# Late output pieces and probability transposes brought together behind the third chunk of a turn

## The reference

```
a = einsum('bqd,bkd->bqk', layernorm(x), ctx)    # ctx: 1 x 25088 x 2048
e = softmax(a, axis=-1)
x = x + einsum('bqk,bkd->bqd', e, ctx)
```

## Time and profile before

| what | value |
|---|---|
| time, median of 3 runs | 2503.16 us (2502.03 to 2505.08) |
| the profiled execution: its time | 2499.3 us |
| the profiled execution: span, first to last instruction | 2497.7 us |
| mean granted clock of TensorE | 0.996 |
| TensorE busy | 2447.4 us, 98% of the span |
| TensorE weight loads | 2008.0 us, 80% |
| VectorE busy | 1944.8 us, 78% |
| GpSimd busy | 1418.9 us, 57% |
| ScalarE busy | 1093.8 us, 44% |
| chain that ended last | 93% TensorE |

### The profile page before, as it was taken

How to read it: one execution, slowest core, us unless ns; L and a number is a source line. 1 busy time by engine, 2 the same in 40 slices (tenths; PEclk the granted TensorE clock), 3 DMA queues, 4 the chain that set the end, 5 groups by cost and what they waited for, 6 DMA issues and landing times.

```text
span 2497.7 us, 36098 instructions
## 1 busy us (share of the span) xinstructions
PE 2447.4 (98%) x11446; PEld 2008.0 (80%) x11446; DVE 1944.8 (78%) x2702; ACT 1093.8 (44%) x1577; POOL 1418.9 (57%) x1056
## 2 busy tenths in 40 slices
PE   6999999999999999999999999999999999999799
PEld 5888888888888888888888888888888888877577
DVE  8788788787888878878788787888888878774356
ACT  4444444444444444444444444444444444333443
POOL 2766666666665665655556556466555655652341
PEclk9999999999999999999999999999999999999899
DMA  9988878888788888888988888888888889779633
GB/s 231 250 222 208 229 204 229 218 207 229 205 230 226 212 212 215 218 220 213 219 213 206 220 218 214 211 217 218 218 214 214 205 218 226 199 165 169 136 121 100
DMA packets 421112, 518.22 MB, mean 207 GB/s; under 512 B 54407, under 2 KB 296071, under 8 KB 418441
## 3 DMA queue, kind: packets, MB, share of 16 engines
q1 hardware_dynamic: 411080, 475.66, 78.1%
q0 software_dynamic: 9984, 41.95, 5.0%
HBM read 488.71 MB, written 28.84 MB: 207 GB/s over the span
## 4 chain that ended last, share of the span: by engine, by line
PE 93%; DMA 2%; DVE 2%; POOL 1%; issue 1%; ACT 1%; SPq 0%; POOLq 0%; ACTq 0%
PE ps L1451 30%; PE ps L1453 30%; PE ps L1452 30%; PE ps L1460 2%; DMA tr<-wt_dram 1%; POOL nat_lo L613 1%; DMA raw<-in_ctx_dram 1%; DMA x_in<-in_x_dram 0%; PE ps L1678 0%; PE ps L1751 0%; PE ps L1624 0%; PE ps L1479 0%; DVE tr L1072 0%; DVE acc L1197 0%; PE ps L1573 0%
## 5 line engine op out<-in xcount | busy, mean ns | idle before, releaser
L613 POOL TENSOR_TENSOR nat_lo<-raw,nat_hi 128x512 fp32r<-128x512 f32 x784 | 1169.7, 1521 | 867.8 <-ACT nat_hi L773 833.8
L1076 DVE TENSOR_TENSOR ch_lo<-tr,ch_hi 128x512 fp32r<-128x512 f32 x784 | 842.3, 1074 | 364.9 <-ACT ch_hi L762 364.8
L762 ACT CAST ch_hi<-tr 128x512 fp32r<-128x512 f32 x784 | 477.5, 621 | 810.3 <-PE ps L1453 804.0
L1451 PE MATMUL ps<-ch_hi,xt_hi 128*128 128x512 f32 x1696 | 678.3, 400 | 11.7 <-DVE ch_lo L1242 5.0
L1453 PE MATMUL ps<-ch_hi,xt_lo 128*128 128x512 f32 x1696 | 664.3, 392 | 0.0
L1452 PE MATMUL ps<-ch_lo,xt_hi 128*128 128x512 f32 x1696 | 663.3, 391 | 0.0
L1451 PE MATMUL ps<-nat_hi,pt_hi 128*128 128x512 f32 x1568 | 611.6, 390 | 4.6 <-DVE pt_lo L1017 4.6
L1453 PE MATMUL ps<-nat_hi,pt_lo 128*128 128x512 f32 x1568 | 610.2, 389 | 0.0
L1452 PE MATMUL ps<-nat_lo,pt_hi 128*128 128x512 f32 x1568 | 610.1, 389 | 0.0
L1072 DVE STREAM_TRANSPOSE tr<-quart 128x512 f32<-128x512 f32 x784 | 547.2, 698 | 1.0 <-DMA quart<-in_ctx_dram 1.0
L773 ACT CAST nat_hi<-raw 128x2048 fp32r<-128x2048 f32 x196 | 374.6, 1911 | 200.8 <-PE ps L1453 189.2
(11 more groups left out here) (200 smaller groups left out, 1312.1 us busy)
## 6 DMA issues: line engine op xcount, KB each, us to landing
quart<-in_ctx_dram SPq DMA_DIRECT2D x392, 512.0 KB, 8.4
raw<-in_ctx_dram SPq DMA_DIRECT2D x196, 1024.0 KB, 8.1
wq_in<-in_L_attn_Wq_dram POOLq DMA_DIRECT2D x16, 1024.0 KB, 6.4
win<-in_L_ffn_W_base_dram SPq DMA_DIRECT2D x64, 256.0 KB, 6.7
tr<-wt_dram POOLq DMA_DIRECT2D x64, 256.0 KB, 3.2
wt_dram<-stage SPq DMA_DIRECT2D x32, 256.0 KB, 5.5
wt_dram<-stage_b SPq DMA_DIRECT2D x32, 256.0 KB, 10.3
wq_dram<-wq_out POOLq DMA_DIRECT2D x16, 256.0 KB, 2.3
```

What stands on the lines that cost most here:

```text
L613: last = pool.tensor_tensor(nat_lo[:, j, t], raw[:, j % 2, t], nat_hi[:, j, t].bitcast(F32), ALU.subtract)
L762: act.copy(ch_hi[:, c % RING_CH, :], tr[:, c % RING_TR, :]).then_inc(chunk_hi, 1)
L1076: dve.tensor_tensor(ch_lo[:, c % RING_CH, :], tr[:, c % RING_TR, :], ch_hi[:, c % RING_CH, :].bitcast(F32), ALU.subtract).then_inc(chunk_s ...
L1451: pe.matmul(out_, a_hi, b_hi, start=start, stop=False)
```

## The change

Late piece 7 moves from behind chunk 3 to behind chunk 2. Both groups of probability transposes stand behind it, one after the other, where before one stood behind chunk 2 and one behind chunk 3 and late piece 7. On ScalarE the two casts to `pt_hi` stand together behind the cast of chunk 6, where before the cast of chunk 7 stood between them. VectorE's list, GpSimd's and SyncE's are unchanged. In the first of the `START` turns, without late pieces, only the groups move. TensorE's list becomes:

```diff
-        LATE_AFTER = {1: 6, 3: 7}
+        LATE_AFTER = {1: 6, 2: 7}
...
                     if c == LEAD and not turn.first:
                         for q in range(TT):
                             softmax(turn, q)
-                    if c in (6, 7) and not turn.first:
-                        probs_group(turn, c - 6)
+                    if c == 6 and not turn.first:
+                        for q in range(TT):
+                            probs_group(turn, q)
                     if c in late:
                         late_row_piece(turn, late[c])
...
                     chunk_scores(turn, c)
                     if c in LATE_AFTER and lagging:
                         late_piece(turn, LATE_AFTER[c])
-                    if c in (2, 3) and not turn.first:
-                        probs_group(turn, c - 2)
+                    if c == 2 and not turn.first:
+                        for q in range(TT):
+                            probs_group(turn, q)
                     if c in PIECE_AFTER and not turn.first:
                         weighted_piece(turn, PIECE_AFTER[c])
```

## The result

The changed kernel took 2552.89 us as a median of four runs (2541.92 to 2555.04), against 2502.60 us before: a ratio of 1.0197 with a 95% interval of 1.0175 to 1.0218. Slower was forecast, at 2542.6 us with a range of 2531 to 2556. The profiled execution took 2541.92 us with a span of 2540.2 us, 42.6 us more than the profiled one of before; 39.4 us had been forecast for that pair.

A forecast was written before the change was run, and what follows sets the result against it. TensorE's instruction stream was taken to bound the steady part; 46 turns at 0.85 us (39.1 us) plus 0.3 us in the second turn gave 39.4 us on 2503.2, so 2542.6 us, range 2531 to 2556.

The forecast's parts named there:

- The stream itself: TensorE's instructions cost the same in the new order; two adjacent groups of transposes take 0.88 us.
- The seam: Joined groups on TensorE save one transposes-to-matmul hand-over, at most 0.09 us per turn, counted as nothing; rival 2499 us, chance 0.02.
- The chain: Chunk 3's end, ScalarE's cast of chunk 7, four VectorE steps, then piece 0: gap 0.85 us per turn; chance 0.78.
- TensorE again: TensorE's restart at piece 0 after group 1's low part: 0.06 us, plus 0.10 us before the second matmul.
- the gap of 0.85: TensorE's wait before piece 0 in each of 46 turns, from 1222.14 to 1222.99.
- 39.1 forecast: Growth of the 46 steady turns in us, at 0.85 us each.
- the upper bound of 1.05: Largest gap per turn before piece 0, with 0.1 us of jitter at each of two hand-overs; gives 2552 us.
- GpSimd's contention: Rival: chunk 7's low part on VectorE takes 1.77 us instead of 0.67 beside GpSimd; 2593 us, chance 0.04.
- The first two turns: First turn with weighted pieces loses nothing; the second, already waiting before piece 0, grows by 0.3 us.
- the gap stays covered: Rival: VectorE's work fits beside chunks 4 and 5, time does not move; 2503 us, chance 0.05.
- The clock: Rival: TensorE's clock falls to 1.2 GHz at the gaps, 1.7 us per turn, 78 us more; 2621 us, chance 0.03.

The follow-up runs named there:

- the low part moved forward: Changed kernel with VectorE's low part of group 1 put before chunk 7's, right behind group 0's: 2498.35 us, ratio 0.9986.
- the reduced wait: Piece 0 waits for group 0's low part only, piece 1 for group 1's: on the changed kernel 0.9962, repeated 0.9973; on the kernel before 0.9984.
- one link less: Changed kernel with VectorE adding late piece 7 behind the low part of group 1 instead of before it: 2521.57 us, ratio 1.0074.
- the late wait last: Changed kernel with TensorE's wait for the low parts put last instead of first of three waits before piece 0: 2541.97 us, ratio 1.0164.
- The repeat: The changed kernel run again with no edit: 2547.76 us, ratio 1.0191.
- two tiny operations in the chain: Changed kernel with the two denominator updates (`rescale`) put before VectorE's low part of group 1: 2713.77 us, ratio 1.0855.

## Why the prediction was right

**The stream itself.** Eight transposes in a row took 0.87 us, as the sum had it. Late piece 7 and the groups waited for nothing. The seam that I counted as nothing is a small gain. Chunks 3 to 5 took 1239.32 + 0.87 to 1244.29, 4.10 us, where the kernel before needed 1.39 + 2.76 = 4.15. In the kernels with the low part moved forward and with the reduced wait, both without a gap, the turns of the loops are 44.41 to 44.45 us, 44.43 on average, instead of 44.49.

**The chain.** Every link was where it had been laid out: the cast 0.26 us behind chunk 3's end (1241.83 against 1241.57), the low part 0.65 us behind the cast's start, then 0.61, 0.62 and 0.63 us, and 0.68 for the last. From the cast's start to the end of `pt_lo` that is 3.19 us against 3.19 forecast. That this chain is the cause is shown from three sides: another order on VectorE, a narrower wait on TensorE, and one link less each gave the time back that it should.

**The term that was mis-sized** is "TensorE again", the restart. I took 0.06 us from the one place where the list of waits has the kernel before waiting here, but that turn is written out. In the loops of the changed kernel it is 0.22 to 0.26 us. The difference of 0.17 us in 44 turns is 7.5 us, and putting the late wait last gave some 7 us back. With it and the 0.05 us less that chunks 3 to 5 take, the gap of 0.85 becomes the measured 1.06.

The trace of the kernel before had this number, which I overlooked. In the first of its two loops VectorE finishes group 1's low part only just in time. These are the rows of one such turn, VectorE's and then TensorE's:

```profile
508.73 0.67 DVE L1017 TENSOR_TENSOR pt_lo<-ps,pt_hi 128x512 fp32r<-128x512 f32 x1
509.33 0.14 DVE L1105 TENSOR_TENSOR denom_s<-denom,alpha 128x2 f32<-128x2 f32 x1
509.50 0.16 DVE L1107 TENSOR_TENSOR denom<-denom_s,row_sum 128x2 f32<-128x2 f32 x1
...
509.65 0.47 PE L1451 MATMUL ps<-nat_hi,pt_hi 128*128 128x512 f32 x1
509.96 0.40 PE L1452 MATMUL ps<-nat_lo,pt_hi 128*128 128x512 f32 x1
```

Piece 0 starts 509.65 - 509.40 = 0.25 us behind the low part's end, and its second matmul comes 0.31 us later instead of 0.23. No idle time shows, since the matmul before still runs in the record, so the list of waits doesn't count it. In 14 turns up to 777 us it is like this, and such a turn is 44.57 to 44.62 us long; with the reduced wait they are 44.49. So the steady part was not wholly without this wait, and 44.49 us is the turn of the second loop only.

**From turns to time.** A turn of the first loop grew from 44.58 to 45.50 us and one of the second from 44.49 to 45.52. The 44 turns of the loops took 1958.9 us before and 2002.4 after, which is 43.5 us more, and the two written out behind them grew by 0.85 us each. That is 45.2 us for the 46 turns, against 39.1 forecast. The two profiled executions differ by 42.6 us, so 2.6 us fell the other way in front of and behind these turns. The ratios 1.0197 and 1.0191 stand for 49 and 48 us; what the executions that were not profiled have on top of the 45.2 stays open.

**Luck at the upper end.** The gap of 1.04 to 1.07 us lies at or above the upper bound of 1.05. The median of 2552.89 us is 0.9 us above the 2552 to which that bound led, and is inside the stated range through the 4 us that were added for GpSimd's contention in a few turns. That contention did not occur. The repeat's 2547.76 us would have been inside without it.

**The first two turns** were not forecast well, and differ between executions. In the first, TensorE waited 1.9 us in one profile of the changed kernel and 4.2 us in the other, against 2.3 before. In the second, where I took a growth of 0.3 us, the gap went from 1.05 to 1.94 us in one and to 0.90 in the other.

**The rivals.** That the gap stays covered fell with the 49 waits. GpSimd's contention did not touch chunk 7's low part (0.69 us), but it was close: GpSimd's piece started at 1244.33, some 1.2 us behind it, and the two operations behind the chain were hit. The clock stayed at 1.00 at gaps of 1.06 us, in both profiles of the changed kernel. It did fall when the gap was made 3.5 us, so this rival was wrong about gaps of 1.06 us, not in kind. The Trainium skill ("TensorE: Matmul & The Clock Gate", A second HAM failure mode: psum-queue depth-cycling) tells of a clock that goes back and forth over short idle stretches between groups of matmuls. The run with two tiny operations in the chain agrees with it (0.83 from 1240 to 1250 us, 1.00 from 1250 to 1291), the changed kernel (1.00 throughout its loops) does not.

## What to carry to other kernels

When a piece of work is moved ahead of another on the busy engine, ask what the one that is pushed back releases elsewhere, and follow that to the next thing the busy engine needs. Here nothing was added and no moved piece was late, yet chunk 3 released a ring slot, and an order on another engine put three unrelated steps between that slot and the operand wanted next. Before a schedule is tuned around a wait, look at whether the wait names more than the data needs: counting one group instead of two took away the whole loss of the changed order. In the kernel before it gave 0.9984, with an interval that reaches 1.0000, and with the changed order 0.9962 and 0.9973. And a list of waits shows only idle time: an operand that arrives just in time can cost a tenth of a microsecond in every turn and stand in no list.

## What was not expected of the hardware

- A wait that ends late costs more when other waits stand behind it in a loop: 0.22 to 0.26 us from the end of the producer to the matmul, against 0.05 to 0.06 with the late wait last. In a loop, put the wait that is expected to end last at the end. In the turns written out the order did the opposite here, 0.05 us with the late wait first and 0.15 with it last.
- What a VectorE operation loses beside GpSimd's subtraction has little to do with its size. The updates of 2 elements a row took 0.14 to 0.16 us alone and 0.68 to 1.22 us beside it, and a low part of 512 elements a row went from 0.67 to 1.77 us. Operations with one input from PSUM were not slowed: the low part of group 1 took 0.68 us with GpSimd's piece running from its start. The Trainium skill ("GPSIMD Engine Reference", 8. Key points) names VectorE instructions with two SBUF inputs as those that contend, and these rows agree. Not each of them is slowed, though: the chunk's low part right behind the updates, at 1246.80 us in the changed kernel, took 0.68 us while GpSimd's piece ran until 1250.43.
- TensorE's clock stayed at 2.4 GHz with a gap of 1.06 us in every turn of 45.5 us, in both profiles of that kernel, and fell to 1.2 GHz, for 7 or 8 matmuls, behind 35 of 43 gaps of 3.5 us.
